# A graph network kernel: late groups turned together with their source terms, one scale for two norms, ScalarE as the engine that normalises

## The reference

```
# layer 0: graph convolution, A = adj + I, d = 1/sqrt(rowsum(A))
An  = d[:, None] * A * d[None, :]
x   = layernorm(x + An @ (relu(An @ (x @ W1) + b1) @ W2) + b2)
# layer 1: graph attention on x
xn  = layernorm(x) * g1 + b1'
for i in range(K):
    h     = xn @ ff0[i].T
    e     = leaky_relu((h @ a_src[i])[:, None] + (h @ a_dst[i])[None, :])
    atten = softmax(where(adj > 0 or on the diagonal, e, -9e15), axis=1)
    att   = layernorm(atten @ h + x) * g2 + b2'
    h_next += elu(att @ ff1[i].T) / K
out = layernorm(x + h_next)
```

## Time and profile before

| what | value |
|---|---|
| time, median of 3 runs | 1020.89 us (1017.95 to 1023.19) |
| time of the profiled execution | 1018.46 us |
| its span in the profile | 1015.4 us |
| mean granted clock of TensorE | 0.987 |
| busy: TensorE | 964.3 us (95%) |
| busy: VectorE | 725.1 us (71%) |
| busy: ScalarE | 492.1 us (48%) |
| busy: GpSimd | 187.1 us (18%) |

### The profile page before, as it was taken

The page is one execution under the profiler, slowest core; times in us unless marked ns, Lnnn a source line. Parts: engine busy times, 40 slices in busy tenths (PEclk is TensorE's granted clock), DMA queues, the critical chain, the costliest instruction groups (busy, mean ns, idle before and its releaser), DMA issues. The chain is left out here.

```text
span 1015.4 us, 9241 instructions
## 1 busy us (share of the span) xinstructions
PE 964.3 (95%) x2492; PEld 453.9 (45%) x2492; DVE 725.1 (71%) x1313; ACT 492.1 (48%) x756; POOL 187.1 (18%) x193
## 2 busy tenths in 40 slices
PE   5988989999999999999999999999999999999993
PEld 4333334444644444444555454444444444444541
DVE  1777766766565443426888777888779999888977
ACT  5343333221200000000088768778676888978774
POOL 1212223233059000004710001000000001010013
PEclk8999999999999999999999999999999999999997
DMA  9999999999579999993232232223212233313311
GB/s 380 419 420 419 418 417 417 415 417 399 243 288 381 379 395 377 387 392 149 87 102 80 65 94 72 94 62 104 68 57 93 84 104 94 104 63 94 94 52 42
DMA packets 69297, 223.88 MB, mean 220 GB/s; under 512 B 5318, under 2 KB 44806, under 8 KB 56710
## 3 DMA queue, kind: packets, MB, share of 16 engines
q1 hardware_dynamic: 65280, 209.67, 54.7%
q10 hardware_dynamic: 3974, 13.73, 3.4%
HBM read 203.43 MB, written 19.96 MB: 220 GB/s over the span
## 5 line engine op out<-in xcount | busy, mean ns | idle before, releaser
L1460 PE MATMUL ps<-T,Yw 128*128 128x512 f32 x1024 | 444.6, 593 | 1.0 <-DVE T L1107 0.6
L1460 PE MATMUL ps<-colbuf,stat 128*128 128x512 f32 x832 | 367.9, 602 | 23.3 <-DVE stat L899 23.3
L1133 DVE SCALAR_TENSOR_TENSOR T<-T,mring 128x2048 f32<-128x2048 f32 x125 | 286.0, 2289 | 63.2 <-ACT T L663 62.6
L663 ACT ACTIVATE T<-Rrow,small,ratio 128x1024 f32<-128x1024 f32 x250 | 294.8, 1231 | 61.5 <-PE ps L1460 61.3
L1460 PEld LDWEIGHTS ps<-T,Yw 128*128 128x128 f32 x1024 | 193.8, 190 | 237.9 <-issue 229.6
L1460 PEld LDWEIGHTS ps<-colbuf,stat 128*128 128x128 f32 x832 | 158.3, 192 | 228.9 <-issue 205.4
L582 ACT ACTIVATE W<-W 128x896 f32<-128x896 f32 (+15 forms) x57 | 67.9, 1191 | 136.1 <-DMA W<-in_adj 135.7
L961 DVE TENSOR_SCALAR mtile<-colbuf 128x4096 uint8<-128x4096 f32 x28 | 65.9, 2355 | 36.9 <-DMA mask<-mtile 36.2
L600 ACT ACTIVATE stat<-xw_g 128x128 f32 x20 | 6.2, 309 | 158.8 <-PE ps L1460 145.8
L524 POOL TENSOR_SCALAR rs<-sumsq 128x4 f32<-128x4 f32 x14 | 15.1, 1078 | 322.6 <-ACT squares L710 322.6
L471 POOL PARTITION_ALL_REDUCE colrow<-W x31 | 33.3, 1075 | 184.8 <-DVE W L860 164.4
(11 more groups left out here) (198 smaller groups left out, 682.5 us busy)
## 6 DMA issues: line engine op xcount, KB each, us to landing
colbuf<-in_adjT SPq DMA_DIRECT2D x64, 1024.0 KB, 16.7
colbuf<-in_adjT SPq DMA_DIRECT2D x24, 2048.0 KB, 10.5
mring<-mask SPq DMA_DIRECT2D x128, 256.0 KB, 2.7
mask<-mtile ACTq DMA_DIRECT2D x26, 512.0 KB, 10.1
W<-in_adjT SPq DMA_DIRECT2D x4, 2048.0 KB, 11.0
Rrow<-s_src SPq DMA_DIRECT2D x9, 512.0 KB, 4.1
W<-in_adj SPq DMA_DIRECT2D x4, 960.0 KB, 15.4
W<-in_adj SPq DMA_DIRECT2D x4, 896.0 KB, 16.0
```

Of the source, the lines that this page charges most:

```text
L663: last = act.activation(T[:, c % TS, j, :], Rrow[:, g % 2, :], ACT.Relu, scale=ratio[:, c * JB + j:c * JB + j + 1], bias=small[:, 8:9])
L1133: v.scalar_tensor_tensor(out=tile, in0=tile, scalar=1.0, in1=mring[:, c % TS, :, :].rearrange("p b n -> p (b n)"), op0=ALU.add, op1=ALU.mu ...
L1460: return pe.matmul(*args, skip_group_check=True, **kw)
```

## The change

- **Turned with the source terms.** Groups 2 to 7 are turned by a full product with `turner`, which is the identity with the four source columns beside it (132 columns). Their blocks need 132 columns of PSUM, so two of a group's four lie in bank k and two in bank k - 2, which group k - 2 must have left. Groups 0 and 1 are turned as before, and their source products follow group 2's sums.
- **One scale.** `comb` = (var * (1 + eps) + eps * eps_all) ** -0.5 is rstd * r2 and scales the source terms in one step. r2 is later made as comb / rstd on VectorE. For the last group GpSimd makes comb first and rstd after it.
- **ScalarE normalises.** x1 = Identity(row * rstd + shift) with shift = -mean * rstd from GpSimd. ScalarE also copies the source terms from PSUM to `raw_st`.
- **Banks.** The z products use three banks (2 to 4) and no longer four (2 to 5), and wait for x1 of groups 4, 5 and 6. Z_FIRST and Z_WAITING stay at 4 and 8.

```diff
-        Z_FIRST, Z_BANKS, Z_WAITING = 4, 4, 8
+        Z_FIRST, Z_BANKS, Z_WAITING = 4, 3, 8
+        TW = P + 2 * K
+        WHOLE = 2
+        OWN_ST = GW - GB * 2 * K
+        def turned(b):
+            k, ib = b // BPG, b % BPG
+            if k < WHOLE:
+                return ps[:, k, cols(ib)]
+            return ps[:, k if ib < 2 else k - 2, ib % 2 * TW:ib % 2 * TW + P]
...
# GpSimd
             def scale_rows(k):
                 pool.wait_ge(moments_ready, k + 1)
                 pstep(pool.tensor_tensor(rstd[:, group(k)], mv[:, group(k), 1], eps_all[:, group(k)], ALU.add))
-                pool.tensor_tensor(rstd[:, group(k)], rstd[:, group(k)], half[:, group(k)], ALU.pow).then_inc(scale_ready, 1)
+                pstep(pool.tensor_tensor(rstd[:, group(k)], rstd[:, group(k)], half[:, group(k)], ALU.pow))
+                pool.tensor_tensor(shift[:, group(k)], neg_mean[:, group(k)], rstd[:, group(k)], ALU.mult).then_inc(scale_ready, 1)
-            def scale_again(k):
...
+            def scale_both(k):
+                pool.wait_ge(moments_ready, k + 1)
...
+                pstep(pool.tensor_scalar(r, mv[:, own, 1], 1.0 + LN_EPS, 0.0, ALU.mult, ALU.add))
+                pstep(pool.tensor_tensor(r, r, eps_both[:, own], ALU.add))
+                pool.tensor_tensor(r, r, half[:, own], ALU.pow).then_inc(comb_ready, 1)
-            for k in range(NG):
+            for k in range(NG - 1):
                 scale_rows(k)
-                scale_again(k)
+                scale_both(k)
+            scale_both(NG - 1)
+            scale_rows(NG - 1)
...
# ScalarE
+            def copy_sources(k):
+                act.wait_ge(stats_ready, k + 1)
+                if k >= WHOLE:
+                    for i, at in enumerate((k, k - 2)):
+                        last = act.activation(raw_st[:, k * BPG + 2 * i:k * BPG + 2 * i + 2, :],
+                                              ps[:, at, 0:2 * TW].rearrange("p (b n) -> p b n", n=TW)[:, :, P:TW], ACT.Copy)
+                    last.then_inc(raw_st_ready, 1)
+            def normalise(k):
+                act.wait_ge(scale_ready, k + 1)
+                for b in range(k * BPG, (k + 1) * BPG):
+                    last = act.activation(x1[:, b, :], turned(b), ACT.Identity, scale=rstd[:, b:b + 1], bias=shift[:, b:b + 1])
+                last.then_inc(x1_ready, 1)
+            for k in range(NG - 1):
...
+                copy_sources(k)
+                normalise(k)
+                if k == 0:
+                    copy_first_sources()
+            copy_sources(NG - 1)
             act.wait_ge(mix_turned, 1)
...
-            for r in range(2, Z_FIRST):
+            read_z(2)
+            normalise(NG - 1)
+            for r in range(3, Z_FIRST):
                 read_z(r)
...
# VectorE
-                last.then_inc(moments_ready, 1)
-            def normalise(k):
...
+                last.then_inc(moments_step, 1)
+                v.wait_ge(moments_step, k + 1)
+                v.tensor_scalar(neg_mean[:, group(k)], mv[:, group(k), 0], -1.0, None, ALU.mult).then_inc(moments_ready, 1)
...
+            v.wait_ge(scale_ready, NG)
+            v.reciprocal(r2[:, :], rstd[:, :]).then_inc(r2_step, 1)
...
# TensorE
             def turn_sums(k):
                 pe.wait_ge(raw_ready, k + 1)
+                if k >= WHOLE:
+                    pe.wait_ge(x1_ready, k - 1)
+                    pe.wait_ge(raw_st_ready, 1)
                 for ib in range(BPG):
-                    last = pe.transpose(ps[:, k, cols(ib)], raw_sums[:, cols(k * BPG + ib)], ident[:, :])
+                    own = raw_sums[:, cols(k * BPG + ib)]
+                    if k < WHOLE:
+                        last = pe.transpose(ps[:, k, cols(ib)], own, ident[:, :])
+                    else:
+                        last = multiply(ps[:, k if ib < 2 else k - 2, cols(ib % 2, TW)], own, turner[:, :], start=True, stop=True)
                 last.then_inc(tr_done, 1)
...
             def multiply_z(r):
                 if r < Z_BANKS:
-                    pe.wait_ge(x1_ready, 2 + r + 1)
+                    pe.wait_ge(x1_ready, 4 + r + 1)
                 else:
                     pe.wait_ge(z_read, r - Z_BANKS + 1)
...
                 late_sums(k, range(LATE // 2, LATE))
-                if k == EARLY - 1:
+                if k == WHOLE:
+                    for own in range(WHOLE):
+                        sources(own)
+                if k == EARLY:
                     pe.wait_ge(early_ready, 1)
-                if k >= 3:
-                    sources(k - 3)
...
-            for k in range(NG - 3, NG):
-                sources(k)
             multiply_z(0)
             multiply_z(1)
...
             multiply_z(2)
+            multiply_z(3)
...
-            multiply_z(3)
+            multiply_z(4)
...
-            for r in range(4, Z_WAITING):
+            for r in range(5, Z_WAITING):
                 multiply_z(r)
```

More of the change, by code:

```diff
@@ L127, in build @@
         rstd = sb("rstd", [P, B], F32)
+        comb = sb("comb", [P, B], F32)
+        eps_both = sb("eps_both", [P, B], F32)
+        neg_mean = sb("neg_mean", [P, B], F32)
+        shift = sb("shift", [P, B], F32)
+        turner = sb("turner", [P, P + 2 * K], F32)
+        raw_st = sb("raw_st", [P, B, 2 * K], F32)
         r2 = sb("r2", [P, B], F32)
@@ L504, in scale_rows @@
                 pstep(pool.tensor_tensor(rstd[:, group(k)], mv[:, group(k), 1], eps_all[:, group(k)], ALU.add))
-                pool.tensor_tensor(rstd[:, group(k)], rstd[:, group(k)], half[:, group(k)], ALU.pow).then_inc(scale_ready, 1)
-            def scale_again(k):
-                pool.wait_ge(scale_ready, k + 1)
+                pstep(pool.tensor_tensor(rstd[:, group(k)], rstd[:, group(k)], half[:, group(k)], ALU.pow))
+                pool.tensor_tensor(shift[:, group(k)], neg_mean[:, group(k)], rstd[:, group(k)], ALU.mult).then_inc(scale_ready, 1)
+            def scale_both(k):
+                pool.wait_ge(moments_ready, k + 1)
                 own = group(k)
[L510 to L514, removed]
-            for k in range(NG):
+                r = comb[:, own]
+                pstep(pool.tensor_scalar(r, mv[:, own, 1], 1.0 + LN_EPS, 0.0, ALU.mult, ALU.add))
+                pstep(pool.tensor_tensor(r, r, eps_both[:, own], ALU.add))
+                pool.tensor_tensor(r, r, half[:, own], ALU.pow).then_inc(comb_ready, 1)
+            for k in range(NG - 1):
                 scale_rows(k)
-                scale_again(k)
+                scale_both(k)
+            scale_both(NG - 1)
+            scale_rows(NG - 1)
             def row_scale(m, part):
@@ L972, in _ @@
             v.wait_ge(consts_ready, 8)
-            v.scalar_tensor_tensor(out=wag[:, :], in0=wag_mean[:, :], scalar=-1.0 / C, in1=wag[:, :],
+            v.scalar_tensor_tensor(out=turner[:, P:TW], in0=wag_mean[:, :], scalar=-1.0 / C, in1=wag[:, :],
                                    op0=ALU.mult, op1=ALU.add).then_inc(centred, 1)
@@ L1006, in stats @@
                 for ib in range(BPG):
-                    last = v.bn_stats(bn[:, k * BPG + ib, :], ps[:, k, cols(ib)])
+                    last = v.bn_stats(bn[:, k * BPG + ib, :], turned(k * BPG + ib))
                 last.then_inc(stats_ready, 1)
@@ L1046, in _ @@
             moments(NG - 1)
[L1047 to L1053, removed]
+            v.wait_ge(raw_st_ready, NG - 1)
+            v.wait_ge(comb_ready, NG)
+            v.tensor_tensor(st[:, :, :], raw_st[:, :, :].rearrange("p b m -> p m b"),
+                            comb[:, :].unsqueeze(1).broadcast_to([P, 2 * K, B]), ALU.mult).then_inc(st_step, 1)
             v.wait_ge(st_step, 1)
[L1055 to L1058, removed]
             v.tensor_tensor(st[:, :, :], st[:, :, :], bcast(s_const[:, :], B), ALU.add).then_inc(st_ready, 1)
@@ L1284, in _ @@
             cap_half_row(1)
+            v.wait_ge(r2_step, 2)
+            v.tensor_tensor(r2[:, :], r2[:, :], comb[:, :], ALU.mult).then_inc(r2_ready, 1)
             set_inside(0, 0, 0)
@@ L1574, in sources @@
                     b = k * BPG + ib
-                    last = multiply(ps[:, 0, cols(b, 2 * K)], raw_sums[:, cols(b)], wag[:, :], start=True, stop=True)
+                    last = multiply(ps[:, 0, OWN_ST + b * 2 * K:OWN_ST + (b + 1) * 2 * K], raw_sums[:, cols(b)],
+                                    turner[:, P:TW], start=True, stop=True)
                 last.then_inc(st_done, 1)
```

52 lines of the change are left out of this document (26 added, 26 removed).

## The result

The changed kernel takes 1032.10 us (median of 4 runs, 1028.27 to 1032.66), the kernel before beside it 1019.58 us (median of 4). The ratio is 1.0097, 95% interval 1.0073 to 1.0120: slower by 1%, inside the predicted range and 1.1 us over the predicted time. The quotient of these two medians of four is larger, 1.0123; the repeat (number 10) has 1.0086. All medians and ratios are of executions in the faster of two states; two of the kernel before beside numbers 9 and 10 (1052.27 and 3649.0 us) were in the slower one and are left out. The profiled execution took 1031.98 us with a span of 1030.2 us.

A forecast was written before the change was run, and what follows sets the result against it. TensorE, busy 964.3 of 1015.4 us, bounds the kernel, without slack behind 523 us. Terms 7.5 + 1.5 + 2.4 = 11.4 take 1018.46 to 1029.9 (1032.3 from the median basis); forecast 1031, range 1026 to 1036.

The forecast's parts named there:

- The wait of pair 7: Ahead of the first chunk, z pair 7 waits for ScalarE's fifth z read, holding TensorE and delaying chunk 1: +7.5 us.
- The fifth read: ScalarE's read of the fifth z pair, after the first relus; forecast to end 10.71 us behind the ratio's start.
- The shift of the ratio: ScalarE's ratio on the reference moves with the later product with top_diag: +1.5 us, bounds -1 and +3.
- The stall at group 0: TensorE waits at the first source products for x1 of group 0, normalised on ScalarE: 1.0 us (0 to 1.4).
- The source products of groups 0 and 1: Moved behind group 2's sums on TensorE, they add 1.6 us there.
- The four periods: TensorE's group periods between group 2's and group 6's turns: 6.08 us each, not 6.49, giving back 1.6.
- The lost cover ahead of the last turn: Source products no longer cover VectorE's add of the features behind group 7's sums, so TensorE waits 0.95 us.
- The clock: TensorE's long idle ahead of pair 7 drops its granted clock to 0.50 behind: +2.4 us, bounds 0 and 4.1.
- Nothing is made good: Behind 523 us TensorE has no slack, so a delay of the first chunks moves the end by as much.
- The hidden wait: Rival: slack behind 523 us or a misplaced read hides pair 7's wait, leaving only 1.5: 1022 us, chance 0.04.
- The wait with a cheaper clock: Rival: pair 7 waits, but the clock costs 1.7 or less or the head is shorter: about 1028 us, chance 0.08.
- The shorter chain for the source terms: Rival: fewer source records and GpSimd steps bring the reference up to 2 us earlier: 1018 us, chance 0.04.

The follow-up runs named there:

- number 10: The changed kernel run again unaltered, against the kernel before: 1030.72 us, ratio 1.0086; its profile is the second profile of the changed kernel.
- numbers 9: Changed kernel with all the joint edits, plus five extra unread products filling TensorE's idle ahead of the first chunk: 1020.47 us, ratio 0.9985 to the kernel before.
- number 5: Changed kernel with Z_WAITING at 7 and VectorE's second mask conversion one group later: 1020.95 us, ratio 0.9995 to the kernel before.
- experiment 2: Kernel before with only Z_BANKS lowered from 4 to 3: 1030.68 us, ratio 1.0084 to the kernel before.
- experiment 4: Changed kernel with Z_FIRST at 5, so ScalarE makes the fifth read ahead of the ratio: 1021.98 us, ratio 1.0005 to the kernel before.
- number 8: Changed kernel with Z_WAITING 6, Z_FIRST 3, later mask conversion, z pair 0 ahead of the last turn and short end: 1020.11 us, ratio 0.9994.
- numbers 7: Changed kernel with Z_FIRST 3, Z_WAITING 6 and a shorter end of the joint (top_diag product not waiting for last x1): 1022.65 us, ratio 1.0016.
- experiments 1 and 6: First: changed kernel with Z_WAITING 7, 1021.65 us, ratio 0.9997. Second: that plus z pair 0 ahead of the last turn, 1021.69 us, ratio 1.0013.

## Why the prediction was right

**The wait of pair 7 (forecast: +7.5 and the shift of the ratio).** Right in place, kind and size. The idle time was forecast at 9 to 11 us and measured at 9.37 in both profiles. Put into the kernel before it gives +0.84% by itself, and taken out of the changed kernel it leaves 0.9997. That it is the cause is shown, from both sides. The fifth read ends 10.70 us behind the start of the ratio (530.69 less 519.99), forecast 10.71.

**The shift of the ratio (+1.5).** From the first turn to the ratio it is 47.25 us before and 49.24 after, of which 0.45 is the first turn at low clock: +1.54. Its parts came out as follows. The stall at group 0 was put at 1.0 and is 0.75 to 0.80; the four normalising instructions take 1.50, where I took 1.65 from the earlier trace rows. The pow takes 2.48 (2.45 before), and 1.06 once no mask conversion starts behind it: number 5 shows that the conversion is what makes it long. The Trainium skill, SBUF — State Buffer, "Who interferes with whom", describes such a lock, and says that the instruction that is issued first has it. The traces agree with the lock and not with the order: the pow starts 0.16 us ahead of the conversion (473.77 and 473.93), and yet it is the pow that becomes long, while the conversion keeps its 2.28. The source products of groups 0 and 1, which stand behind group 2's sums, ran 16 records in 1.81 (478.25 to 480.06), forecast 1.6. The four periods from group 2's turn to group 6's take 24.32 us (482.71 to 507.03), forecast 24.3. The lost cover ahead of the last turn was put at 0.95, of which 0.78 stands as a wait. The last turn starts 40.24 us behind the first in the second profile, 38.58 before: +1.7, forecast +1.5. The product with top_diag comes at +1.57, forecast +1.5.

**The clock (+2.4, bounds 0 and 4.1).** The right mechanism, a little low: from pair 7 to the pair behind chunk 2 the work is 0.90 + 3 x 3.47 = 11.3 us. It took 14.19 and 13.93 in the changed kernel (+2.9, +2.6), 13.28 in experiment 2 (+2.0), and 11.26 with the wait filled (0). In the windows of after the clock is 0.50 for 5.6 us, within the forecast of 4 to 8. In the times the filled wait is worth 1.0068 against 1.0097 and 1.0086; those intervals overlap, so it is the trace that shows it.

**Nothing is made good.** The forecast rested on the earlier trace rows. From the pair behind chunk 2 to the end it is 485.26 us, 485.40 before.

**The sum.** 7.5 + 1.5 + 2.4 = 11.4 against 12.4 (with the 0.45) and 11.7 in B. In the times it is less: ratios of 1.0097 and 1.0086 are some 10 and 9 us. The sum started from a profile that is quicker than most executions of its kernel, and the forecast of 1031, set between that basis and the median, lies between the two measured medians, 1032.10 and 1030.72. That it comes so close is partly luck: the place was chosen between two bases that lay 2.4 us apart. The later first turn of the one profile, 2.5 us, cannot be laid to the change: experiment 2 has it at 470.59 with the program of before up to there, and experiment 4 at 468.11 with the changed one.

**The rivals.** The hidden wait fell with the timeline. The wait with a cheaper clock (1.7 or less) is ruled out by the two profiles of the changed kernel, 2.9 and 2.6; the times alone (the repeat is some 9 us over the kernel before) would leave it open. The shorter chain for the source terms did not come to pass: st is scaled 45.16 us behind the first turn (515.91; 44.7 without the 0.45), 43.97 before (512.22), as the later last turn takes more than GpSimd's common scale saves. The rival also counted wrongly: GpSimd has six steps for a group before and six after, not seven and six; what it gains is only that the common scale comes first for the last group. In number 8, with the other waits around it gone, the product with top_diag comes 0.4 us earlier than before (A 45.87); the end of the first column group does not.

## What to carry to other kernels

A buffer count is a distance between two programs. Where it is lowered, look at each place where the producer runs ahead by a number that was chosen for the old count (here: pairs ahead of the first chunk = early reads + banks), and ask what is queued behind the one that now waits. And an idle time of TensorE ahead of a stage that it bounds may be worth filling: products that nobody reads brought back 2.6 to 2.9 us behind the long wait. Behind the short one (numbers 8 and 9) B is 0.8 and D 0.6 us shorter with them, but a gain in the time (0.9994 and 0.9985) is not shown. Last, before a distance in a profile is compared between kernels, count what work has been moved across its end, as with B above.

## What the runs showed of the hardware

- The granted clock fell to 0.50 behind idle times near and below the 2.20 us of the earlier trace rows, but not each time. In numbers 7 and 8 TensorE was empty for 2.6 us, in number 5 for 1.80 us, ahead of chunks that took 12.07, 12.07 and 12.19 us instead of 11.30; experiments 1 and 6, with 1.81 us at the same place, kept 1.00. A wait of 2.35 to 2.37 us near 785 to 800 us is in all twelve profiles (the second row of the waits above); in ten the eight records behind it take 2.00 us, and in numbers 7 and 8 they take 2.77 and 2.88. Which execution has it, these profiles do not tell.
- It fell with hardly any idle as well. In experiment 2 the clock is 1.00 in the first part of the last 24 records of 4 columns (twelve source products) and 0.50 behind, with TensorE busy all along; the product with top_diag came 3.1 us later for it (A 49.41 against 46.30). The profile of before has the same records and kept 1.00. Three of the seven profiles of the new joint that have a wait of 0.8 us and then sixteen records of 4 columns show the low clock behind them, at a cost of 1.7 us each. So a profile in which TensorE is busy does not by itself say that its clock was high.

```profile
508.00:511.50 3.50, 3.50 (x31) 3.19 (x29) 2.69 (x13) 0.38 (x1) 2.31 (x6) 1.00 0.49 147
512.00:517.50 5.50, 5.50 (x19) 4.78 (x19) 3.08 (x12) 1.53 (x4) 2.13 (x5) 0.50 0.24 83
```

- Four Identity activations of 128x128 with a scale and a bias per row take 1.50 us from PSUM and 1.65 from SBUF.
